# Cross-attention and a routed feed-forward layer on one core: part of the up-weight preparation on GpSimd, and the last square sum of the down weights later on ScalarE

## What is computed

```python
kv = k_v @ W_k.T + b_k
out = jnp.einsum('bij,bjd->bid', p, kv)
sim = jnp.einsum('bid,bjd->bij', out, kv) * scale
sim = (sim - mu) * jax.lax.rsqrt(var + EPS) * ln_gamma + ln_beta
x = x + softmax(sim)
```

```python
for e in range(E):
    h = silu(einsum('btd,hd->bth', x, W1[e])) * einsum('btd,hd->bth', x, W2[e])
    y = y + w[..., e:e + 1] * einsum('bth,dh->btd', h, W3[e])
```

## Time and profile before

| | before |
|---|---|
| median of 3 runs | 374.2 us |
| profiled execution | 373.96 us, span 371.8 us |
| busy over the span | PE 94%, DVE 67%, ACT 71%, POOL 47% |
| granted TensorE clock, mean | 0.977 |
| largest groups on the chain that ended last | PE L1297 37%, PE L1333 20% |

### The profile page before, as it was taken

One profiled execution on the slowest core, in us unless ns is written; L12 is line 12 of the kernel. 1 busy time (PEld: TensorE's weight loads), 2 busy tenths in 40 slices (PEclk: granted clock), 3 DMA queues, 4 the chain that ended last, 5 costly groups with the idle time before them and its releaser, 6 DMA issues.

```text
span 371.8 us, 8177 instructions
## 1 busy us (share of the span) xinstructions
PE 351.3 (94%) x2284; PEld 230.1 (62%) x2284; DVE 250.3 (67%) x554; ACT 264.4 (71%) x451; POOL 175.5 (47%) x243
## 2 busy tenths in 40 slices
PE   8999999998989999999999999999999999999980
PEld 7555676777656555566666666666666666666640
DVE  2367688978979999976565666656565747475740
ACT  2478999995999899957575757566666666666640
POOL 2134846778631546544444435363535454545331
PEclk9999999999669999999999999999999999999997
DMA  6999999999730344445454545445454545453524
GB/s 217 416 412 409 333 417 416 357 341 396 236 89 0 59 86 63 82 87 91 81 89 85 85 89 84 89 74 100 70 104 66 104 69 107 63 99 70 87 32 53
DMA packets 21944, 57.70 MB, mean 155 GB/s; under 512 B 4816, under 2 KB 4944, under 8 KB 20368
## 3 DMA queue, kind: packets, MB, share of 16 engines
q0 software_dynamic: 8736, 20.61, 32.0%
q1 hardware_dynamic: 12016, 30.30, 21.5%
q10 hardware_dynamic: 1152, 6.29, 4.6%
HBM read 38.25 MB, written 18.94 MB: 154 GB/s over the span
## 4 chain that ended last, share of the span: by engine, by line
PE 76%; DVE 5%; DMA 5%; issue 4%; ACT 4%; POOL 3%; POOLq 1%; SPq 1%; ACTq 0%; DVEq 0%
PE bank L1297 37%; PE bank L1333 20%; PE bank L1288 4%; DMA Wp<-in_w 3%; PE bank L1317 3%; PE bank L1154 3%; PE bank L1085 2%; PE bank L1200 1%; DMA out<-kvj_s,sidx 1%; PE bank L1174 1%; PE bank L1127 1%; ACT Wp L646 1%; DVE Wp L870 1%; PE bank L1183 1%; POOL rstd L439 1%
## 5 line engine op out<-in xcount | busy, mean ns | idle before, releaser
L1032 DVE SCALAR_TENSOR_TENSOR stage<-W,w3sc,stage 128x512 f16<-128x512 f16 x117 | 84.2, 748 | 6.1 <-ACT stage L698 6.1
L1333 PE MATMUL bank<-stage,n_s 128*128 128x512 f16 (+1 forms) x351 | 82.2, 379 | 4.7 <-issue 3.3
L698 ACT ACTIVATE stage<-W,w3sc 128x512 f16 x117 | 80.1, 718 | 0.0
L1297 PE MATMUL bank<-Wp,kvg_s 128*128 x480 | 78.2, 312 | 0.9 <-DVE kvg_s L1038 0.9
L1297 PE MATMUL bank<-Wp,kv_s 128*128 x456 | 74.3, 312 | 0.4 <-DVE kv_s L1038 0.4
L1048 DVE TENSOR_TENSOR n_s<-bank,n_s 128x384 f16<-128x384 f32 x39 | 21.7, 557 | 68.2 <-ACT n_s L713 68.2
L1297 PEld LDWEIGHTS bank<-Wp,kvg_s 128*128 128x128 f16 x480 | 46.7, 98 | 26.7 <-issue 1.8
L1297 PEld LDWEIGHTS bank<-Wp,kv_s 128*128 128x128 f16 x456 | 44.3, 98 | 25.4 <-issue 2.1
L539 POOL DMA_INDIRECT out<-oT_s,sidx x20 | 32.1, 1606 | 57.0 <-ACT oT_s L729 53.4
L518 POOL DMA_INDIRECT ng_s<-n_table,gidx x39 | 43.2, 1108 | 32.1 <-POOL wm L532 22.7
L1333 PEld LDWEIGHTS bank<-stage,n_s 128*128 128x128 f16 (+1 forms) x351 | 33.8, 97 | 38.9 <-issue 6.1
(11 more groups left out here) (198 smaller groups left out, 529.4 us busy)
## 6 DMA issues: line engine op xcount, KB each, us to landing
Wp<-in_w SPq DMA_DIRECT2D x8, 1408.0 KB, 10.3
W<-in_w ACTq DMA_DIRECT2D x8, 768.0 KB, 7.3
stage<-in_xT SPq DMA_DIRECT2D x4, 1024.0 KB, 8.9
W<-in_x SPq DMA_DIRECT2D x12, 256.0 KB, 9.7
out<-W SPq DMA_DIRECT2D x12, 256.0 KB, 8.8
n_table<-n_s SPq DMA_DIRECT2D x8, 256.0 KB, 7.8
n_table<-x_s SPq DMA_DIRECT2D x8, 256.0 KB, 7.7
stage<-in_x SPq DMA_DIRECT2D x4, 256.0 KB, 8.7
```

Of the source, the lines that this page charges most:

```text
L698: eng.activation(w3p[t % 2][:, c * D:(c + 1) * D], W3[:, bass.ds(e * W3N + c * D, D)], ACT.Copy, scale=w3sc[:, bass.ds(e, 1)]).then_inc(s_ ...
L1032: eng.scalar_tensor_tensor(w3p[r][:, W3N + c * D:W3N + (c + 1) * D], W3[:, bass.ds(e * W3N + c * D, D)], w3sc[:, bass.ds(e, 1)], w3p[r][:, ...
L1297: mm = eng.matmul(bank[2 * which + r][:, 0:H], n_, w_, start=(c == 0 and k == 0), stop=(c == DC - 1 and k == 2))
L1333: mm = eng.matmul(ybank(t - 1)[:, :], h_, w_, start=(c == 0 and k == 0), stop=(c == HC - 1 and k == 2))
```

## The change

GpSimd gets ten new instructions on 128x1408 elements. For experts 2, 4 and 6 it makes the up half in three steps: scale the raw weights in place, copy them as float16 to the high half, subtract to the low half. For expert 1 it makes the high half in one step. The pieces of expert 1 and 2 stand behind the first three gathers, those of 4 and 6 between gathers and scatters of tiles 0 to 4. ScalarE and VectorE skip these halves: ScalarE does four instructions fewer, VectorE three. ScalarE does the last square sum of the down weights behind `mT_evac(0)`, where the high parts of expert 1 stood, and the first of these high parts before it. VectorE makes the low parts of expert 1 ahead of the scale of the down weights. The counts of `s_hi` and `s_lo` are adjusted, and `s_pw` counts GpSimd's pieces. The semaphores of the down weights' loads are now one for two experts.

```diff
+POOL_LOW = (2, 4, 6)
+POOL_HIGH = (1,) + POOL_LOW
+POOL_PIECES = (("high", 1), ("scale", 2), ("high", 2), ("low", 2), ("scale", 4), ("high", 4), ("low", 4), ("scale", 6), ("high", 6), ("low", 6))
...
-        s_w3 = [sem(f"s_w3_{i}") for i in range(E)]
+        s_w3 = [sem(f"s_w3_{i}") for i in range(PAIRS)]
+        s_pw = sem("s_pw")
...
+        def high_count(k, h):
+
+            return 2 * k + h + 1 - sum(j < k or (j == k and h == 1) for j in POOL_HIGH)
...
+        def pool_count(piece, k):
+
+            return POOL_PIECES.index((piece, k)) + 1
+
+        def low_ready(eng, k, h):
+
+            if h == 1 and k in POOL_LOW:
+                eng.wait_ge(s_pw, pool_count("low", k))
+            else:
+                eng.wait_ge(s_lo, low_count(k, h))
...
+            def second_half(k):
+
+                cols = slice(WH, 2 * WH)
+                high = Wp[:, 2 * k * W12N:(2 * k + 1) * W12N]
+                low = Wp[:, (2 * k + 1) * W12N:(2 * k + 2) * W12N]
+                return wst[k][:, cols], high[:, cols], low[:, cols]
+
+            def scaled_high(k):
+
+                raw, high, low = second_half(k)
+                eng.wait_ge(s_wsc, 1)
+                low_ready(eng, k - 1, 0)
+                eng.tensor_scalar(high, raw, wscale[:, k:k + 1], None, ALU.mult).then_inc(s_pw, 1)
+
+            def scale_half(k):
+
+                raw, high, low = second_half(k)
+                eng.wait_ge(s_wsc, 1)
+                eng.tensor_scalar(raw, raw, wscale[:, k:k + 1], None, ALU.mult).then_inc(s_pw, 1)
+
+            def high_half(k):
+
+                raw, high, low = second_half(k)
+                low_ready(eng, k - 1, 0)
+                eng.wait_ge(s_pw, pool_count("scale", k))
+                eng.tensor_copy(high, raw).then_inc(s_pw, 1)
+
+            def low_half(k):
+
+                raw, high, low = second_half(k)
+                low_ready(eng, k - 1, 1)
+                eng.wait_ge(s_pw, pool_count("high", k))
+                eng.tensor_tensor(low, raw, high, ALU.subtract).then_inc(s_pw, 1)
+
             gather(0)
             gather(1)
             gather(2)
+            scaled_high(1)
+            scale_half(2)
+            high_half(2)
+            low_half(2)
...
                 row_weights(t)
                 gather(t + 3)
+                if t == 0:
+                    scale_half(4)
+                if t == 1:
+                    high_half(4)
+                if t == 2:
+                    low_half(4)
+                if t == 3:
+                    scale_half(6)
+                    high_half(6)
+                if t == 4:
+                    low_half(6)
...
-                if k >= E:
+                if k >= E or h == 1 and k in POOL_HIGH:
                     return
...
             w3_square(2)
-            w3_square(3)
+            w12_high(1, 0)
...
             mT_evac(0)
-            w12_high(1, 0)
-            w12_high(1, 1)
+            w3_square(3)
...
-                if k >= E:
+                if k >= E or h == 1 and k in POOL_LOW:
                     return
-                eng.wait_ge(s_hi, 2 * k + h + 1)
-                wait(eng, s_lo, 2 * k)
+                if h == 1 and k in POOL_HIGH:
+                    eng.wait_ge(s_pw, pool_count("high", k))
+                else:
+                    eng.wait_ge(s_hi, high_count(k, h))
+                if k > 0:
+                    low_ready(eng, k - 1, 1)
...
             low_rows(0)
+            w12_low(1, 0)
+            w12_low(1, 1)
             w3_sums()
             w3_scale()
-            w12_low(1, 0)
-            w12_low(1, 1)
...
                     if t < E:
-                        eng.wait_ge(s_lo, 2 * t + 1)
+                        low_ready(eng, t, 0)
...
                     if t < E:
-                        eng.wait_ge(s_lo, 2 * t + 2)
+                        low_ready(eng, t, 1)
```

More of the change, by code:

```diff
@@ L317, in ring_free, with low_count @@
                 eng.wait_ge(s_S, G)
+        def high_count(k, h):
+            return 2 * k + h + 1 - sum(j < k or (j == k and h == 1) for j in POOL_HIGH)
+        def low_count(k, h):
+            return 2 * k + h + 1 - sum(j < k or (j == k and h == 1) for j in POOL_LOW)
+        def pool_count(piece, k):
[5 more added lines that the diff above has]
+                eng.wait_ge(s_lo, low_count(k, h))
         def ybank(t):
@@ L622, in w3_square @@
                 e = W3_ORDER[2 * k]
-                eng.wait_ge(s_w3[e], 16)
-                eng.wait_ge(s_w3[e + 1], 16)
+                eng.wait_ge(s_w3[e // 2], 16 * 2)
                 wait(eng, s_w3q, k)
@@ L655, in w12_high @@
                     eng.wait_ge(s_wq, 2 * E)
-                wait(eng, s_lo, 2 * k - 1)
+                else:
+                    low_ready(eng, k - 1, 0)
                 eng.activation(Wp[:, 2 * k * W12N + h * WH:2 * k * W12N + (h + 1) * WH], wst[k][:, h * WH:(h + 1) * WH],
@@ L666, in weight_loads @@
                         eng.wait_ge(s_n, (e + 1) * W3N // D)
-                    eng.dma_start(W3[:, e * W3N:(e + 1) * W3N], w3[e]).then_inc(s_w3[e], 16)
+                    eng.dma_start(W3[:, e * W3N:(e + 1) * W3N], w3[e]).then_inc(s_w3[e // 2], 16)
             eng.wait_ge(s_bk, 16)
```

## The result

**391.73 us** (median; 390.72 to 392.89), against 374.33 us for the kernel before on the same chip: ratio **1.0466**, 95% interval 1.0437 to 1.0494, so 17.4 us slower. The forecast was 384, range 376 to 390. The direction held, and VectorE was held by GpSimd as forecast; the size fell outside the range. The profiled execution has a span of 389.6 us, 17.8 above the 371.8 of before.

A forecast was written before the change was run, and what follows sets the result against it. VectorE was taken to set the pace in tiles 1 to 6, with GpSimd's pieces excluding it for 21.6 us; seven steps summed to +10.15 on the profiled 373.96, giving 384 us, range 376 to 390.

The forecast's parts named there:

- Step 1: Ahead of tile 0: the later last square sum delays the small matmul to about 112.5 and the first gate product, +1.6.
- Step 2: Up to tile 0's down product: GpSimd's pieces for experts 1 and 2 exclude VectorE; down product at 126.1, +3.05.
- the small steps on the down scale run under it: Before tile 1's low rows: VectorE's small scale operations (0.75) run beneath GpSimd's copy for expert 2.
- Step 3: Tiles 1 and 2: one low half gone, expert 4's scaling loses 0.7, TensorE bounds tile 2; -0.65 in the sum.
- Step 4: Tile 3: expert 4's subtraction holds `w3_low` chunk 0 ahead of `low_rows(4)`, delaying tile 4's gate product, +3.85.
- Step 5: Tile 4: a low half saved (-1.6), but expert 6's scaling and copy exclude 3.5, partly beneath one-input work; -0.15.
- Step 6: Tile 5: expert 6's subtraction holds `w3_low` chunk 0 to 160.1, gate product 6 at 162.0, +3.1.
- Step 7: Tile 6 and after: no GpSimd piece left, TensorE bounds, 6.29 against 6.96 in tile 6; -0.65.
- is not last in any of these tiles: Early tiles: ScalarE is never the last producer, so its four dropped high halves are worth nothing by themselves.
- rival A: GpSimd's long pieces do not hold VectorE, notably at `w3_low` of tiles 3 and 5: 372.3 us, not slower; chance 0.14.
- B: Same exclusion but cheaper pieces, 1.2 to 1.4 per one-input piece, some hidden: +4.4, 378.3 us; chance 0.16.
- C: TensorE's clock falls after idle times ahead of its first product and at tiles 4 and 6: about +4, 388; chance 0.12.

The follow-up runs named there:

- experiment 2: Kernel before with GpSimd and VectorE operations added behind the last scatter, on idle engines, to price each by itself; its own time (432.35) means nothing.
- experiment 3: Changed kernel with GpSimd's ten pieces replaced by fills of about the same length that read nothing; 378.62 us, ratio 1.0118.
- experiment 4: Changed kernel with TensorE kept busy by extra matmuls ahead of the small matmul and of tiles 1 and 2's gate products; 392.21 us, ratio 1.0464.
- experiment 5: Kernel before, GpSimd zero fills replacing experts 2 to 7's low up halves (373.58 us), high halves (375.59) or both (371.55).
- experiment 1: Kernel before with the changed order on ScalarE and VectorE alone, no pieces on GpSimd; 377.60 us, ratio 1.0078.

## Why the prediction was right, and where it was wrong

The core of the mechanism was right: GpSimd's long pieces do shut VectorE out, for up to 3.6 us at a time, and what they hold first of all is VectorE's operations with two SBUF inputs. The Trainium skill, "SBUF — State Buffer", section "Who interferes with whom", says that a VectorE instruction with two SBUF inputs contends with a GpSimd instruction that reads SBUF and not with one that only writes it; experiment 2 agrees with both (3.32 beside the subtraction, 0.75 beside a fill). The prediction was incomplete in that one-input steps in SBUF are held as well, even by fills (experiments 2 and 3). The total held by luck, 21.6 predicted and 21.1 measured. What failed is how it is made up and how much of it the path sees: 10.15 predicted, 18.1 measured by tile 8. By steps, which measured add up to that 18.1:

- **Step 1** (+1.6): the square sum was right (small matmul at 112.50). The first product starts 1.1 behind it, not 0.35: **+2.3**.
- **Step 2** (+3.05) is the main mis-sized term, and the step that failed most: **+6.4** measured. The scaling was priced 1.76 from a two-scalar row and holds VectorE for about 2.4 to 3.6; copy and subtraction were priced 1.76 and 3.1 and hold for 1.0 and 2.6. The clause "the small steps on the down scale run under it" put them at no cost, and was wrong: they are held for 3.6 in all, eight columns like 512. The down product comes at 130.13 instead of 126.1, of which 2.3 are the two scalings (`w12_low(1,1)` ends at 118.2, not 115.9) and most of the rest is the late scale, which `w3_high` and `w3_low` need.
- **Step 3** (-0.65): wrong in sign, **+4.1**. 0.7 was counted for expert 4's scaling, most of it behind `low_rows(2)`; it holds 3.6 ahead of it. And "TensorE bounds tile 2" was wrong: 8.38 us, 1.4 of it the clock (experiment 4), the rest the second chain.
- **Step 4** (+3.85): wrong in the other direction, **-0.1**. By then everything was later, the subtraction fell 0.5 us behind `low_rows(4)` and cost 0.8 in the next tile; the gate products of tiles 4 and 6 have none of the idle time that the prediction named as its sign. The prediction itself said that a start that is 1 us off moves a piece to the other side.
- **Step 5** (-0.15): **+0.8**, which is that subtraction.
- **Step 6** (+3.1): **+3.8**, near in size, but by luck: not the subtraction does it, but the scaling, which holds the `w12_low` in front of the up product for 2.9, and the copy, which holds the `w3_low` behind it for 1.1.
- **Step 7** (-0.65): tile 6 takes 7.73 because of the subtraction, **+0.8**; the 6.29 come one tile later.

The view that misled was the busy time of the earlier trace rows: VectorE at 6.63 to 6.83 of 6.95 looked like the pace-setter alone, and ScalarE at 6.0 to 6.5 like slack. ScalarE "is not last in any of these tiles" was wrong (experiments 3 and 5). The change relieves VectorE in even windows and ScalarE in odd ones, so even without holding it wins nothing: in experiment 3 tiles 2 to 5 still take 6.88 to 6.95, and the time is 378.6 where rival A gave 372.3. Of the other rivals, B had the pieces cheaper (only copy and subtraction were; its sign, a copy under 1.5, came with 1.36, its time did not), C had a part of the clock right and not its worth.

What adds up, by medians: order about 3.3, waits for the pieces themselves about 1.0 (experiment 3 less 1), holding 13.1. The scaling's form is some 8 of the whole. The first three are uncertain by 2 us or more, as the intervals of experiments 1 and 3 say, and waits and holding overlap.

## What to carry to other kernels

Price an instruction from a row of exactly its form, with the same number of operands: here the one-scalar multiply cost 2.5 times the two-scalar one. Before an engine is relieved, look for a second chain of equal length by what each producer's last instruction waits for, not by busy shares; in this kernel relief of VectorE alone left the tile at 6.96, and relief of both brought it to 6.29. And when GpSimd takes work beside VectorE, list every VectorE instruction that it can hold, the tiny ones too, and ask who reads their result.

## What the runs showed of the hardware that I had not expected

- GpSimd's multiply of 1408 columns by one per-partition scalar takes 3.83 us, with two scalars 1.51, a copy 1.36. The Trainium skill, "GPSIMD Engine Reference", section "Engine selection", calls one-input work roughly line-rate; experiment 2 agrees for copy and two-scalar form (estimate by the page 1.2) and not for the one-scalar form.
- An operation of VectorE on 8 columns, with one input in SBUF, waits as long as one on 512: it takes 2.35 (experiment 2) and 2.75 us (changed kernel) beside a subtraction, and 1.29 beside a fill (experiment 3).
- Beside a subtraction VectorE's own work begins about 0.2 us ahead of the recorded end of GpSimd's instruction (3.32 less 0.75, from 401.34, against 404.11), beside the one-scalar multiply 0.86 ahead (4.61 less 1.68, from 157.39, against 161.18).
- The lower clock cost nothing in three of four tiles with 0.74 to 0.84 granted, since TensorE was not the last one there. Where it was, in tile 0 of experiment 1, 0.70 cost 1.15 us.
